# Turning the norms of the attention's steps by DMA, one tile a step, instead of by TensorE

## What is computed

```
x = x + 0.5 * ffn(layernorm(x))          # norm k = 0, FFN f = 0
x = x + attention(layernorm(x))          # norm k = 1
x = x + 0.5 * ffn(layernorm(x))          # norm k = 2, FFN f = 1

attention: q = n @ Wq (32 heads of 128), k, v = n @ Wk, n @ Wv (8 groups); rope(q), rope(k)
           softmax(causal(q k^T / sqrt(128))) v  per head, then @ Wo + bo
ffn(n):    router scores and attention over 128 slots, top 8, softmax, slot values (two low-rank products)
           times a gate made of var(n) and gelu(n @ Wu1.T + bu1) @ Wu2.T;  returns n + gate * aux
```

## Time and profile before

| | |
|---|---|
| median of 3 runs | 1498.8 us (1497.66 to 1503.31) |
| the profiled execution, its own time | 1500.57 us |
| its span in the trace | 1498.3 us |
| TensorE busy | 1393.6 us, 93% of the span |
| VectorE busy | 1229.7 us, 82% |
| ScalarE busy | 875.4 us, 58% |
| GpSimd busy | 531.1 us, 35% |
| DMA queue of SP | 56.0% of 16 engines' span |

### The profile page before, as it was taken

The page is one execution under the profiler, slowest core; times in us unless marked ns, Lnnn a source line. Parts: engine busy times, 40 slices in busy tenths (PEclk is TensorE's granted clock), DMA queues, the critical chain, the costliest instruction groups (busy, mean ns, idle before and its releaser), DMA issues.

```text
span 1498.3 us, 26151 instructions
## 1 busy us (share of the span) xinstructions
PE 1393.6 (93%) x8832; PEld 795.5 (53%) x8962; DVE 1229.7 (82%) x3107; ACT 875.4 (58%) x2166; POOL 531.1 (35%) x440
## 2 busy tenths in 40 slices
PE   5578999998999999999999998999999999999965
PEld 4344554554555655555555654555555555555533
DVE  6777979998988977989787987889778888888744
ACT  3367676666665665556655665565655656555623
POOL 0375655655542232233422322323323333323102
PEclk9799999999999999999999999999999999999988
DMA  6158767768765555555554644565555565655413
GB/s 228 42 148 193 190 161 168 192 168 190 165 148 108 135 129 107 126 127 120 124 138 106 141 121 98 120 136 117 130 130 138 137 137 125 141 118 124 100 31 112
DMA packets 409555, 201.12 MB, mean 134 GB/s; under 512 B 352176, under 2 KB 353392, under 8 KB 409424
## 3 DMA queue, kind: packets, MB, share of 16 engines
q1 hardware_dynamic: 407312, 195.25, 56.0%
q10 hardware_dynamic: 2112, 4.19, 0.8%
HBM read 90.30 MB, written 25.17 MB: 77 GB/s over the span
## 4 chain that ended last, share of the span: by engine, by line
PE 67%; DVE 16%; ACT 7%; issue 4%; POOL 3%; DMA 1%; SPq 1%; DVEq 0%; ACTq 0%
PE PJ L1096 16%; PE PJ L1097 15%; PE PJ L1095 14%; PE PV L1095 3%; PE PV L1097 3%; PE PV L1096 3%; PE SC L1254 3%; PE SC L1255 3%; PE SC L1256 3%; DVE phl L910 3%; ACT p L584 3%; POOL t L453 3%; DVE p L899 2%; DVE t L872 2%; DVE t L871 1%
## 5 line engine op out<-in xcount | busy, mean ns | idle before, releaser
L453 POOL TENSOR_TENSOR t<-t 128x512 f32<-128x512 f32 x160 | 203.3, 1271 | 714.0 <-DVE t L872 713.8
L584 ACT ACTIVATE p<-p,mn 128x512 f32<-128x512 f32 (+3 forms) x512 | 281.0, 550 | 185.6 <-DVE mn L899 185.5
L910 DVE SCALAR_TENSOR_TENSOR phl<-p,ri,phl 128x512 f16<-128x512 f32 (+3 forms) x512 | 303.8, 616 | 0.0
L593 ACT ACTIVATE phl<-p,ri 128x512 f16<-128x512 f32 (+3 forms) x512 | 244.6, 550 | 18.9 <-DVE ri L1006 16.9
L1095 PE MATMUL PJ<-XTh,wsp 128*128 128x512 f16 x640 | 243.4, 380 | 3.7 <-DVE t L872 2.3
L1096 PE MATMUL PJ<-XTl,wsp 128*128 128x512 f16 x640 | 243.1, 380 | 0.0
L1097 PE MATMUL PJ<-XTh,wsp 128*128 128x512 f16 x640 | 243.1, 380 | 0.0
L899 DVE CUSTOM_DVE_ANT_0 p<-SC,maskw 128x512 f32<-128x512 f32 (+3 forms) x512 | 219.7, 485 | 2.9 <-PE SC L1256 0.6
L1096 PE MATMUL PJ<-wosp,oTf 128*128 128x512 f16 x512 | 196.0, 383 | 10.9 <-DVE raw L751 5.7
L1097 PE MATMUL PJ<-wosp,oTl 128*128 128x512 bf16 x492 | 188.3, 383 | 0.0
L456 POOL TENSOR_TENSOR qTl<-t,qTh 128x512 f16<-128x512 f32 x128 | 148.3, 1159 | 95.0 <-ACT qTh L566 95.0
(11 more groups left out here) (187 smaller groups left out, 2573.7 us busy)
## 6 DMA issues: line engine op xcount, KB each, us to landing
wsp<-kept SPq DMA_DIRECT2D x144, 256.0 KB, 2.9
wosp<-kept SPq DMA_DIRECT2D x96, 256.0 KB, 3.3
raw<-in_wqkv SPq DMA_DIRECT2D x48, 256.0 KB, 4.8
kept<-wsp SPq DMA_DIRECT2D x48, 256.0 KB, 2.3
raw<-in_wo SPq DMA_DIRECT2D x32, 256.0 KB, 5.0
pTf<-phl SPq DMA_TRANSPOSE x512, 2.9
kept<-wosp SPq DMA_DIRECT2D x32, 256.0 KB, 2.9
X<-in_x ACTq DMA_DIRECT2D x4, 1024.0 KB, 11.1
```

What stands on the lines that cost most here:

```text
L453: nc.gpsimd.tensor_tensor(t1[:, j, :], t1[:, j, :], t2[:, j, :], ALU.add).then_inc(rope_sum, 1)
L584: ins = nc.scalar.activation(pt, pt, ACT.Exp, bias=mn[:, par, i:i + 1], scale=-1.0, accum_out=rs[:, par, i:i + 1])
L593: nc.scalar.activation(phl[:, par, POFF[i]:POFF[i] + w], p[:, par, SOFF[i]:SOFF[i] + w], ACT.Copy, scale=ri[:, par, i:i + 1]).then_inc(a_p ...
L910: nc.vector.scalar_tensor_tensor(out=phl[:, par, POFF[i] + w:POFF[i] + 2 * w], in0=p[:, par, SOFF[i]:SOFF[i] + w], scalar=ri[:, par, i:i + 1],
```

## The change

Inside the steps a norm tile is no longer turned by TensorE. ScalarE writes the high half of the float32 norm, still in token order, into a staging buffer in SBUF (the even tiles into `asc`, the odd ones into a new buffer `hl`); VectorE writes the low half behind it; one DMA transpose from SP's queue turns both halves (128 x 1024 float16) straight into the turned buffer `XT` (`XF` for norm 2). The float32 norm is in `hb` for all tiles. The consumers (`SCR`, `HID`, the K projection) wait on the DMA's semaphore. The 36 tiles are taken one a step: `nrm` and `hi` of tile i in one step, `lo` and the transpose in the next. The first `nrm` of a batch stays in its step (u = 0, 22 and 8). The `LT` tasks leave `RING`, so the banks are dealt out anew. The head and the tail are as before.

```diff
-PE_A = {2: [("LT", 0, 0), ("LT", 0, 1)], 4: [("LT", 0, 2), ("LT", 0, 3)], 6: [("SCR", 0, 0)], 8: [("SCR", 0, 1)],
-        10: [("HID", 0, 0)], 12: [("HOUT", 0, 0), ("ET", 0, 0)], 18: [("AUX", 0, 0), ("AUX", 0, 1)],
-        20: [("AUX", 0, 2), ("AUX", 0, 3)], 24: [("LT", 1, 0), ("LT", 1, 1)], 26: [("LT", 1, 2), ("LT", 1, 3)]}
-PE_B = {12: [("LT", 2, 0), ("LT", 2, 1)], 14: [("LT", 2, 2), ("LT", 2, 3)], 16: [("SCR", 1, 0)], 22: [("SCR", 1, 1)],
-        28: [("HID", 1, 0)], 30: [("ET", 1, 0), ("HOUT", 1, 0)]}
+PE_A = {6: [("SCR", 0, 0)], 8: [("SCR", 0, 1)], 10: [("HID", 0, 0)], 12: [("HOUT", 0, 0), ("ET", 0, 0)],
+        18: [("AUX", 0, 0), ("AUX", 0, 1)], 20: [("AUX", 0, 2), ("AUX", 0, 3)]}
+PE_B = {16: [("SCR", 1, 0)], 22: [("SCR", 1, 1)], 28: [("HID", 1, 0)], 30: [("ET", 1, 0), ("HOUT", 1, 0)]}
...
-DVE_A = {0: [("nrm", 0, 0), ("nrm", 0, 1)], 2: [("lo", 0, 0), ("lo", 0, 1), ("nrm", 0, 2), ("nrm", 0, 3)],
-         4: [("lo", 0, 2), ("lo", 0, 3)], 6: [("scr", 0, 0)], 7: [("top", 0, 0)], 8: [("scr", 0, 1)],
+DVE_A = {0: [("nrm", 0, 0)], 1: [("lo", 0, 0), ("nrm", 0, 1)], 2: [("lo", 0, 1), ("nrm", 0, 2)],
+         3: [("lo", 0, 2), ("nrm", 0, 3)], 4: [("lo", 0, 3)], 6: [("scr", 0, 0)], 7: [("top", 0, 0)], 8: [("scr", 0, 1)],
...
-         22: [("std", 1, 0), ("nrm", 1, 0), ("nrm", 1, 1)],
-         24: [("lo", 1, 0), ("lo", 1, 1), ("nrm", 1, 2), ("nrm", 1, 3)], 26: [("lo", 1, 2), ("lo", 1, 3)]}
-DVE_B = {6: [("var", 2, 0)], 8: [("std", 2, 0), ("nrm", 2, 0), ("nrm", 2, 1)],
-         12: [("lo", 2, 0), ("lo", 2, 1), ("nrm", 2, 2), ("nrm", 2, 3)], 14: [("lo", 2, 2), ("lo", 2, 3)],
+         22: [("std", 1, 0), ("nrm", 1, 0)], 23: [("lo", 1, 0), ("nrm", 1, 1)], 24: [("lo", 1, 1), ("nrm", 1, 2)],
+         25: [("lo", 1, 2), ("nrm", 1, 3)], 26: [("lo", 1, 3)]}
+DVE_B = {6: [("var", 2, 0)], 8: [("std", 2, 0), ("nrm", 2, 0)], 9: [("lo", 2, 0), ("nrm", 2, 1)],
+         10: [("lo", 2, 1), ("nrm", 2, 2)], 11: [("lo", 2, 2), ("nrm", 2, 3)], 13: [("lo", 2, 3)],
...
+SP_A = {1: [("turn", 0, 0)], 2: [("turn", 0, 1)], 3: [("turn", 0, 2)], 4: [("turn", 0, 3)],
+        23: [("turn", 1, 0)], 24: [("turn", 1, 1)], 25: [("turn", 1, 2)], 26: [("turn", 1, 3)]}
+SP_B = {9: [("turn", 2, 0)], 10: [("turn", 2, 1)], 11: [("turn", 2, 2)], 13: [("turn", 2, 3)]}
...
+            def turn_normal(k, bb, i):
+                both = XF if k == 2 else XT[:, bb % 2, :, :]
...
+                sp.wait_ge(ln_lo[k], 4 * bb + i + 1)
+                sp.dma_start_transpose(both[:, :, lo_slice(i)], halves_of(k, i)).then_inc(ln_x[staging(k, i)], 16)
...
                 if s:
                     turn(s - 1)
+                for _, k, bb, i in side(SP_A, SP_B, s):
+                    turn_normal(k, bb, i)
...
+            def normal_hi(k, bb, i):
+                f = 0 if k < 2 else 1
+                act.wait_ge(ln_h[k], 4 * bb + i + 1)
...
+                nc.scalar.copy(halves_of(k, i)[:, 0:C], normal_of(k, bb, i)).then_inc(ln_hi[k], 1)
...
+            def normal_lo(k, bb, i):
+                both = halves_of(k, i)
+                dve.wait_ge(ln_hi[k], 4 * bb + i + 1)
+                nc.vector.tensor_tensor(both[:, C:2 * C], normal_of(k, bb, i), both[:, 0:C],
+                                        ALU.subtract).then_inc(ln_lo[k], 1)
```

More of the change, by code:

```diff
@@ L183, in macaron_kernel @@
         hb = sb("hb", [P, 2, C], F32)
+        hl = sb("hl", [P, 2 * C], F16)
         fwq = oTf[0:BOT, 0:C]
@@ L225, in macaron_kernel @@
         ld_t, st_out = sem("ld_t"), sem("st_out")
+        ln_x = {where: sem(f"ln_x{where}") for where in ("hl", 0, 1)}
         ld_r = [sem(f"ld_r{k}") for k in range(NRAW)]
@@ L326, in xt_of, with by_pe, staging, halves_of @@
         def xt_of(k, bb):
-            return (XF[:, 0, :, :], XF[:, 1, :, :]) if k == 2 else (XTh[:, bb % 2, :, :], XTl[:, bb % 2, :, :])
+            both = XF if k == 2 else XT[:, bb % 2, :, :]
+            return both[:, 0:CC, :], both[:, CC:2 * CC, :]
+        def by_pe(k, bb):
+            return bb == 0 if k < 2 else bb == B - 1
         def normal_of(k, bb, i):
-            if (k < 2 and bb == 0) or (k == 2 and bb == B - 1):
-                return pTf[:, i * C:(i + 1) * C]
-            f = 0 if k < 2 else 1
+            return pTf[:, i * C:(i + 1) * C] if by_pe(k, bb) else hb[:, i % 2, :]
+        def staging(k, i):
+            return "hl" if i % 2 else (0 if k < 2 else 1)
+        def halves_of(k, i):
             if i % 2:
-                return asc[:, f, :, :].rearrange("p t n -> p (t n)")
-            return hb[:, f, :]
+                return hl[:, :]
+            return asc[:, 0 if k < 2 else 1, :, :].rearrange("p t n -> p (t n)").bitcast(F16)
+        turns = {"hl": [], 0: [], 1: []}
+        hb_users = ([], [])
+        for s_ in range(NS):
+            for _, k_, b_, i_ in side(SP_A, SP_B, s_):
+                turns[staging(k_, i_)].append((k_, b_, i_))
+                hb_users[i_ % 2].append((k_, b_, i_))
+        def landed(k, bb, i):
+            where = staging(k, i)
+            return ln_x[where], 16 * (turns[where].index((k, bb, i)) + 1)
         def e_of(f, bb):
@@ L389, in turn @@
                                            phl[:, par, POFF[i]:POFF[i] + 2 * w]).then_inc(p_turned[par][i], 16)
+            def turn_normal(k, bb, i):
+                both = XF if k == 2 else XT[:, bb % 2, :, :]
+                if i == 0:
+                    if k == 0 and bb >= 2:
+                        sp.wait_ge(s_q, 4 * G * (bb - 1))
+                    if k == 1:
+                        sp.wait_ge(u_ps[0], bb + 1)
+                        sp.wait_ge(r_sc[0], 2 * bb + 2)
+                    if k == 2:
+                        sp.wait_ge(w_lo, len(ITEMS))
+                        if bb:
+                            sp.wait_ge(u_ps[1], bb)
+                            sp.wait_ge(r_sc[1], 2 * bb)
+                sp.wait_ge(ln_lo[k], 4 * bb + i + 1)
+                sp.dma_start_transpose(both[:, :, lo_slice(i)], halves_of(k, i)).then_inc(ln_x[staging(k, i)], 16)
             sp.wait_ge(ld_x[2], 16)
@@ L644, in _ @@
                     if stage == "hi":
-                        turned_hi(k, bb, i)
+                        normal_hi(k, bb, i)
                     if stage == "xup":
@@ L1101, in free, with turned @@
                     pe.wait_ge(*consumed(BEFORE[task]))
+            def turned(k, bb, i):
+                if by_pe(k, bb):
+                    pe.wait_ge(ln_lo[k], (0 if k < 2 else 4 * bb) + i + 1)
+                else:
+                    pe.wait_ge(*landed(k, bb, i))
             def turn_tile(k, bb, i):
@@ L1113, in score_tiles @@
                 hi, lo = xt_of(2 * f, bb)
-                pe.wait_ge(ln_lo[2 * f], 4 * bb + 2 * j + 2)
+                turned(2 * f, bb, 2 * j)
+                turned(2 * f, bb, 2 * j + 1)
                 for t in range(2):
@@ L1124, in hidden @@
                 hi, lo = xt_of(2 * f, bb)
-                pe.wait_ge(ln_lo[2 * f], 4 * bb + 4)
+                for i in range(TB):
+                    turned(2 * f, bb, i)
                 for c in range(CC):
@@ L1196, in project @@
                 out_ = bank(task)
-                xh, xl = XTh[:, b % 2, :, :], XTl[:, b % 2, :, :]
+                xh, xl = xt_of(1, b)
                 if n % G == 0 and kind == "K":
-                    pe.wait_ge(ln_lo[1], 4 * b + 4)
+                    for i in range(TB):
+                        turned(1, b, i)
                 if kind in "QK":
```

64 lines of the change are left out of this document (29 added, 35 removed).

## The result

The changed kernel takes **1487.41 us** in the median of 4 runs (1486.82 to 1488.21), the kernel before 1501.05 us beside it (1497.66 to 1503.32): a ratio of 0.9908, 95% interval 0.9889 to 0.9928. It is faster by 13.6 us where 26.9 were forecast, so about half of the forecast gain came, though 1487.41 lies within the range of 1458 to 1490. The profiled execution took 1487.66 us, its span 1485.6.

The account below looks back on a forecast made before the run. TensorE was taken to bound nearly every step from 28 on, VectorE to set the pace in batch 0's loaded steps. 12.3 + 10.0 + 5.6 - 1.0 = 26.9 us off gave a median of 1472 us, 8-in-10 range 1458 to 1490.

Parts of the forecast that it names:

- 14 LT pairs, steps 34 to 110: TensorE-bound steps of batches 1 to 3: each LT pair that leaves saves 0.88 us, 12.3 us in all.
- the stalls of steps 44 and 76, with 0.6 us of 45 and 77: Steps 44 and 76: with LT out of the ring of banks, 10.0 of 10.3 us of stall and slow clock go.
- VectorE and ScalarE, batches 1 to 3: VectorE's work spread differently around steps 40, 41 and 72: 1.0 us charged; ScalarE's `hi` waiting for `nrm`: nothing.
- batch 0, steps 0 to 33: VectorE's waits for `hi` go, 7.2 us, less 1.6 us for a dearer `lo`: 5.6 us off.
- TensorE as the bound of batches 1 to 3: From step 28 on nearly every step is as long as its TensorE work, so TensorE time removed comes off.
- I cost it at nothing: ScalarE: `hi` waiting for `nrm` of the same step costs nothing; uncovered, under 0.5 us a tile, 18 us at most.
- Where VectorE leads it comes off the time: Batch 0: VectorE's waits for `hi`, 1.79 us for each of 4 pairs, come off the time, 7.2 us.
- Steps 24 to 27, which were to lose 3 us: Batch 0, sign that the forecast is right: these steps, 48.90 us before, get shorter by 3 us or more.
- Cost zero: SP's queue: 36 more transposes cost no time; the bad end is 1.26 us for each tile, 45 us.
- One more issue fits: SP's queue: 2.5 us idle in a busy stretch leaves room for one more transpose issue of 1.26 us.
- Rival 1: VectorE: each `lo` waits for a whole GpSimd instruction, 1.27 us; only 12 us gained, 1487; chance 0.14.
- Rival 2: SP's queue: each added issue delays the probability transposes and so `attend`; 18 us slower, 1517; chance 0.07.

Follow-up runs that it names:

- Experiment 5: Changed kernel with only `hi` moved behind the K or V half of its step on ScalarE; 1482.25 us, 0.9861 of the kernel before.
- experiment 4: Changed kernel with `hi` one step after `nrm`, `lo` and the transpose one more step later; 1477.41 and, once more, 1481.23 us.
- experiment 14: Kernel of experiment 4 with the eight `lo` of batch 0 replaced by clearing the low half; 1477.46 us.
- 11: Kernel of experiment 4 with batch 0's eight norm transposes left out, their tiles replaced by one plain copy; 1478.00 us.
- 6: Kernel of experiment 4 with `lo` moved ahead of the rope multiplies on VectorE; 1483.04 us.
- 8: Kernel of experiment 4 with each norm transpose issued as two halves on SP; 1489.10 us.

## Why the prediction was right or wrong

| term | forecast us | measured us |
|---|---|---|
| 14 LT pairs, steps 34 to 110 | -12.3 | -12.3 |
| the stalls of steps 44 and 76, with 0.6 us of 45 and 77 | -10.0 | -10.7 |
| steps 38 and 70, not forecast | 0 | -1.3 |
| VectorE and ScalarE, batches 1 to 3 | +1.0 | +8.05 |
| batch 0, steps 0 to 33 | -5.6 | +2.3 |
| sum | -26.9 | -14.0 |

The profiles' steps 0 to 126 went from 1344.6 to 1330.6 us, which is 14.0; the medians differ by 13.6.

**TensorE as the bound of batches 1 to 3: right.** 0.88 us came off in each of the twelve ordinary steps with a pair, and both long steps are as sized. TensorE's waits for `lo` in them went with the `LT` tiles, which fits the reading of the ring of banks.

**"I cost it at nothing" (ScalarE's `hi` behind `nrm`): the step that failed in batches 1 and 2.** The new stalls are 1.00, 1.97, 1.03, 1.00, 1.97 and 1.08 us in steps 47, 57, 59, 79, 89 and 91. I had weighed when `nrm` and rope's copy meet, with `lo` and `nrm` at the durations that they have alone, and found the wait under 0.5 us a tile. It was 0.83 in the mean of 30 and 3.23 at worst, because `lo` collided with GpSimd in nearly every tile (33 of 36 took 1.25 us or more) and `nrm` in some (median 0.54 us, longest 1.51, 10 of 36 over 0.6). And I named what stands behind `hi`, but not that VectorE waits for it in turn: VectorE, `nrm`, ScalarE, V's half, VectorE is a loop between two engines inside a step. Experiment 5 breaks it and gets 4.5 of the 8.05 us back, experiment 4 gets 6.0 to 6.2. What the last 2 us are stays open.

**"Where VectorE leads it comes off the time" (batch 0): failed.** The step that failed is to count 4 x 1.79 us of VectorE's waits for `hi` as time: the waits went, and the stretch got 2.3 us longer. Steps 24 to 27, which were to lose 3 us, took 52.80 instead of 48.90. That VectorE was 42.36 us busy of 48.90 and that TensorE waited for turned probabilities did not make VectorE the bound: experiment 14 takes 8 us off it and no time. With neither SP's eight transposes nor `hi` in the step of `nrm` (11), steps 0 to 33 took 366.1 us against 368.4 before, 2.3 less. The eight issues add 0.8 to 1.5 (4 against 11), and the places of `hi`, `lo` and the transpose add 3.1 to 3.8 (changed against 4). Of this, 2.6 go with the place of `hi` alone (5). How that reaches the time in batch 0 isn't shown: ScalarE waited for `nrm` only 3.1 us in these eight tiles. Nor is all of batch 0 the change's own steps: those got 5.5 us longer (203.5 to 209.0), and steps 7 to 21 got 3.2 shorter, unexplained.

**"Cost zero" (SP's queue): no sign against it in batches 1 to 3, 0.8 to 2.2 us too low over batch 0, and 2.8 to 4.5 in the steps around the issues.** "One more issue fits" was nearly true over the whole, and a second one didn't fit: 3.4 and 7.1 to 7.9 us. What holds the queue in some turns of batch 0, up to 9.1 us for four issues, stays open; the norm transposes alone don't, since the kernel before has it too. What bounds batch 0 is therefore not shown, only that it isn't VectorE's `lo`.

**Rival 1 had the time, 1487, and not the mechanism, so its hit is luck.** `lo` did take 1.25 us, which is 0.57 us more than alone, where the rival let it wait 1.27 us. By itself its length cost nothing that could be measured: 4 and 5 keep it and gain, 6 and 14 take it away from 4 and don't. In the changed kernel it also stands ahead of `nrm` in the loop, and no run separates its share there. Rival 2 was right in kind for a second issue, not for the first.

Kernel 4, the same change with `hi` a step later, is faster than both: 0.9830 and 0.9859 of before in two measurements, against 0.9908. In its steps it lies 23.8 and 23.3 us below before, some 3 us from the forecast.

## What to carry to other kernels

When an instruction moves between engines, follow the whole loop: not only who waits for it, but whether the engine that it waits for will wait for what stands behind it. A producer and a consumer of two engines belong in different steps when both have slack in whole steps and none within one. And a high busy share beside a wait doesn't name the bound; taking work off that engine tests it. Sum such a test over the steps that it touches and over the rest apart: here steps that held nothing of the edit moved by 3 us.

## What was not expected of the hardware

- The collision with GpSimd belonged to a place in VectorE's order more than to an instruction: with `lo` moved away (6) it fell from 1252 to 683 ns, and `nrm`, which took its place, grew from 821 to 1018 ns in the mean.
- An SP issue of a DMA transpose took 1.23 to 1.31 us in the median for 128 x 1024 and 1.27 us for 128 x 512, so splitting one into two doubled the queue's time for it (2.57 and 2.58 us for two in a row in 8).
- In steps 24 to 27 the granted clock fell from 1.00 to 0.90 in the changed kernel, where TensorE's waits for turned probabilities were longer too (8.9 us against 5.9). TensorE was 43.89 us busy with 253 matmul records, against 41.58 us with 266 before.
